# Prologue of a gated cross-attention and expert kernel: first chunk in halves, x in eight loads, one normalisation a unit sooner

## The reference, cut to what matters

```python
x = x + tanh(g_xattn) * xattn(layernorm(x), ctx, Wq, Wk, Wv, Wo, bo)     # 16 heads of 64, softmax over 128 keys
x = x + tanh(g_ffn) * ffn(layernorm(x), gate_w, gate_bias, experts, shared)
# ffn: sigmoid scores of 32 experts, best 2 of 4 groups, best 8 experts in them, weights normalised times 2.5;
#      every expert is silu(x Wg) * (x Wu), then Wd; one shared expert of twice the width is added
```

## Time and profile before

| | |
|---|---|
| runs, median of 3 | 667.44 us (667.02 to 667.79) |
| profiled execution | 668.55 us, of which the span from first to last instruction 666.8 us |
| PE busy | 650.9 us (98%) |
| DVE busy | 498.9 us (75%) |
| ACT, POOL busy | 365.3 us (55%), 284.6 us (43%) |
| granted TensorE clock | 0.999 |
| chain that ended last | PE 68%, issue 8%, DMA 6%, DVE 6%, SP's queue 5% |

### The profile page before, as it was taken

The page is one execution under the profiler, slowest core; times in us unless marked ns, Lnnn a source line. Parts: engine busy times, 40 slices in busy tenths (PEclk is TensorE's granted clock), DMA queues, the critical chain, the costliest instruction groups (busy, mean ns, idle before and its releaser), DMA issues.

```text
span 666.8 us, 13629 instructions
## 1 busy us (share of the span) xinstructions
PE 650.9 (98%) x3668; PEld 473.2 (71%) x3668; DVE 498.9 (75%) x1331; ACT 365.3 (55%) x690; POOL 284.6 (43%) x316
## 2 busy tenths in 40 slices
PE   8999999999999999999999999999999999999997
PEld 6656656667666666666657778788887878888785
DVE  6989858677586776776787968969596877869565
ACT  3564555465455555555465455555655655555553
POOL 4222323133132322234212655656565666657553
PEclk9999999999999999999999999999999999999999
DMA  8323322232323323233224825273654527374550
GB/s 188 94 64 82 92 63 70 63 91 63 80 62 79 94 62 79 62 79 83 63 67 130 192 62 134 83 170 99 141 133 98 134 72 164 81 162 112 131 142 16
DMA packets 63276, 65.58 MB, mean 98 GB/s; under 512 B 26112, under 2 KB 41600, under 8 KB 63232
## 3 DMA queue, kind: packets, MB, share of 16 engines
q1 hardware_dynamic: 63232, 65.07, 40.0%
HBM read 61.64 MB, written 2.88 MB: 97 GB/s over the span
## 4 chain that ended last, share of the span: by engine, by line
PE 68%; issue 8%; DMA 6%; DVE 6%; SPq 5%; POOL 4%; ACT 2%; DVEq 0%; POOLq 0%; ACTq 0%
PE bank L1151 13%; PE bank L1152 13%; PE bank L1153 13%; PE bank L1227 9%; PE bank L1251 5%; POOL halves L516 4%; PE bank L1187 3%; DMA inverse_bc<-inverse_dram 3%; PE bank L1207 2%; SPq L294 2%; DMA sums<-area 2%; DVE halves L783 2%; PE bank L1216 2%; PE bank L1213 2%; PE bank L1210 2%
## 5 line engine op out<-in xcount | busy, mean ns | idle before, releaser
L516 POOL TENSOR_TENSOR halves<-area,halves 128x512 fp32r<-128x512 f32 x134 | 173.9, 1298 | 141.3 <-ACT halves L650 137.8
L663 ACT ACTIVATE area<-bank 128x512 f32<-128x512 f32 x136 | 81.4, 599 | 116.1 <-PE bank L1153 115.1
L602 ACT ACTIVATE area<-bank 128x512 f32<-128x512 f32 x128 | 69.5, 595 | 118.7 <-PE bank L1216 118.7
L1107 DVE TENSOR_TENSOR bank<-area,bank 128x512 f32<-128x512 f32 x128 | 88.6, 692 | 53.4 <-PE bank L1153 53.2
L1227 PE MATMUL bank<-area,ctx_keys 128*65 128x512 f32 (+1 forms) x256 | 124.7, 600 | 0.5 <-ACT u_odd L550 0.4
L1151 PE MATMUL bank<-x2t_hi,w_hi 128*128 128x512 f32 x272 | 110.2, 405 | 0.1
L1152 PE MATMUL bank<-x2t_hi,w_lo 128*128 128x512 f32 x272 | 107.2, 394 | 0.0
L1153 PE MATMUL bank<-x2t_lo,w_hi 128*128 128x512 f32 x272 | 106.3, 391 | 0.0
L462 POOL TENSOR_TENSOR ctx_hi<-ctx_raw,ones_col 128x128 fp32r<-128x128 f32 x32 | 19.7, 615 | 200.4 <-DMA ctx_raw<-ctx_t 200.4
L792 DVE TENSOR_REDUCE row_max<-bank 128x4 f32<-128x512 f32 x128 | 81.7, 680 | 27.2 <-PE bank L1187 22.9
L650 ACT ACTIVATE halves<-area 128x512 fp32r<-128x512 f32 x136 | 85.0, 625 | 14.1 <-DVE area L1118 13.6
(11 more groups left out here) (129 smaller groups left out, 1088.1 us busy)
## 6 DMA issues: line engine op xcount, KB each, us to landing
wbc<-rows_dram SPq DMA_DIRECT2D x126, 256.0 KB, 4.4
inverse_bc<-inverse_dram SPq DMA_DIRECT2D x64, 256.0 KB, 3.9
w_raw<-experts SPq DMA_DIRECT2D x32, 102.0 KB, 2.0
ctx_raw<-ctx_t SPq DMA_DIRECT2D x32, 64.0 KB, 1.8
ctx_keys<-ctx_nat SPq DMA_DIRECT2D x32, 64.0 KB, 2.1
out<-area SPq DMA_DIRECT2D x7, 256.0 KB, 3.9
max_rows<-max_t SPq DMA_DIRECT2D x64, 4.0 KB
area<-wq_t SPq DMA_DIRECT2D x1, 512.0 KB, 4.6
```

The costliest lines, as they stand in the source:

```text
L516: nc.gpsimd.tensor_tensor(hid_lo[:, u % SLOTS, :], hid[:, u % HIDS, :], raw(hid_hi[:, u % SLOTS, :]), ALU.subtract).then_inc(hidlo_ready, 1)
L602: nc.scalar.activation(probs_t[:, k, :, :], st_ps[q][:].rearrange("p (h n) -> p h n", h=4), ACT.Exp)\
L663: nc.scalar.activation(silu_g[:, u % 2, :], gate_ps[u % 2][:], ACT.Silu).then_inc(silu_ready, 1)
L1107: nc.vector.tensor_tensor(up_ps[u % UPS][:], silu_g[:, u % 2, :], up_ps[u % UPS][:], ALU.mult)\
```

## The change

Six edits go together.

1. Layouts in DRAM: x and out are held with the partition first, so that a chunk is 2 KB in a row for each partition (before, four pieces of 512 bytes); wq and wo likewise.
2. Query and key weights come in two halves of four pairs with a semaphore each, the key half's first DMA behind the first memset alone.
3. The normalised chunk 0 goes through `apply`, transpose, `xt_high` and `xt_low` in two halves of two batches; the halves use banks 6 and 7. `g_project(0, ...)` runs banks 0 and 1, then the second half's transposes, then banks 2 and 3.
4. The first fold of value and output weights stands right behind `transpose_max(0, 0)`, the second behind its wait for `maxt_ready`; before, both stood behind `max_scores(1, ...)`. The statistics of chunk 1 are begun before the maxima of batch 1 and ended behind them. The gates' tanh and the gated bias stand behind `g_high(0, ...)` on ACT.
5. x comes in eight loads, with a semaphore each: 1 to 3 behind the router's weights, 4 behind the first two weight loads (which now stand behind the first `max_rows`), 5 and 6 in chunk 0 behind `spread_inverse(0)`, 7 behind `spread_inverse(1)`.
6. `normalise` of batch 31 moves from units 9 and 10 to units 8 and 9.

```diff
+X_AT = {1: (5, 6), 2: (7,)}
-NORM_AT = {(9, 1): ((NB - 1, 0),), (10, 1): ((NB - 1, 1),)}
+NORM_AT = {(8, 1): ((NB - 1, 0),), (9, 1): ((NB - 1, 1),)}
 fold_ps = (bank[0], bank[2])
+xt_ps = bank[6:8]
 # SP
+            def load_x(n):
+                tiles = slice(CB * n, CB * n + CB)
+                sp.dma_start(x_sb[:, tiles, :], x[:, tiles, :]).then_inc(x_in[n], 16)
-            sp.dma_start(x_sb[:, 0:CB, :], x_dram[:, 0:CB, :]).then_inc(x_in[0], 16)
-            sp.dma_start(wq_pair, wq_t.rearrange("(p r) n -> r p n", r=P)).then_inc(wqk_in, 16)
+            load_x(0)
+            for h in range(2):
+                sp.dma_start(wq_pair[:, pairs_of(h), :], wq_t[:, pairs_of(h), :]).then_inc(wqk_in[h], 16)
+                if h == 0:
+                    sp.wait_ge(zeroed, 1)
+                for q in range(2):
+                    load_diag(wk_diag, wk_t, q, pairs_of(h), wqk_in[h])
+            load_raw(0, 0)
             sp.wait_ge(zeroed, 2)
...
-            sp.dma_start(x_sb[:, CB:NB, :], x_dram[:, CB:NB, :]).then_inc(x_in[1], 16)
+            for n in range(1, 4):
+                load_x(n)
+            sp.wait_ge(const_ready, 1)
+            load_max_row(0, 0, -2)
             for slot in range(2):
                 load_weights(slot, slot * WSTEP)
-            sp.wait_ge(const_ready, 1)
-            load_max_row(0, 0, -2)
+            load_x(4)
 # SP, attention, behind spread_inverse
+                    if first:
+                        for n in X_AT.get(b, ()):
+                            load_x(n)
 # POOL
-            pool.wait_ge(x_in[1], 16)
 # ACT
             a_high(0)
-            xt_high(0)
+            xt_high_half(0)
             a_high(1)
+            g_high(0, 0, range(2))
+            xt_high_half(1)
+            g_high(0, 0, range(2, 4))
...
-            g_high(0, 0)
 # DVE
-            ln_apply(0, 0)
+            dve.wait_ge(rstd_step[0], RSTD_STEPS)
+            apply(0, 0, range(2))
             a_low(0)
-            xt_low(0)
+            xt_low_half(0)
+            apply(0, 0, range(2, 4))
             a_low(1)
-            g_low(0, 0)
+            g_low(0, 0, range(2))
+            xt_low_half(1)
+            g_low(0, 0, range(2, 4))
...
             g_low(1, 1)
+            chunk_stats_begin(1)      # waits for x_in[1]
...
-            dve.wait_ge(x_in[1], 16)
-            chunk_stats(1)
+            chunk_stats_end(1)
 # PE
-            pe.wait_ge(wqk_in, 16 * 3)
+            pe.wait_ge(wqk_in[0], 16 * 3)
             fold(wq_pair, wk_diag, 0, fold_ps[0])
             pe.wait_ge(const_ready, 6)
-            transpose_norm(0, ut_ps)
+            transpose_half(0)
+            pe.wait_ge(wqk_in[1], 16 * 3)
             fold(wq_pair, wk_diag, 1, fold_ps[1])
-            g_project(0, 0, ((glo_ready, -2), (glo_ready, -2)))
+            g_project(0, 0, None, range(2))
+            transpose_half(1)
+            g_project(0, 0, None, range(2, 4))
+            pe.wait_ge(xlo_ready, 1)
...
             transpose_max(0, 0)
+            pe.wait_ge(wvo_in, 16 * 3)
+            fold(wv_diag, wo_pair, 0, early_ps[0][0][0])
             pe.wait_ge(maxt_ready, 1)
+            fold(wv_diag, wo_pair, 1, early_ps[0][0][1])
...
-            pe.wait_ge(wvo_in, 16 * 3)
-            pe.wait_ge(max_ready, 2)
-            for i in range(2):
-                fold(wv_diag, wo_pair, i, early_ps[0][0][i])
 # host: x and out as (P, NB, D), wq and wo by pair
```

More of the change, by code:

```diff
@@ L176, in build @@
         fold_ps = (bank[0], bank[2])
+        xt_ps = bank[6:8]
         early_ps = ((bank[6:8], bank[4:6]), (bank[0:2], bank[4:6]))
         gate_ps, up_ps, route_ps, y_ps, misc_ps = bank[0:2], bank[2:5], bank[5], bank[6], bank[7]
-        x_in = [sem("x_in0"), sem("x_in1")]
-        wqk_in, wvo_in, small_in, router_in = sem("wqk_in"), sem("wvo_in"), sem("small_in"), sem("router_in")
+        x_in = [sem(f"x_in{n}") for n in range(NCH)]
+        wqk_in = [sem("wqk_in0"), sem("wqk_in1")]
+        wvo_in, small_in, router_in = sem("wvo_in"), sem("small_in"), sem("router_in")
         keys_in = [sem(f"keys_in{b}") for b in range(CB)]
@@ L530, in xt_high, with xt_high_half @@
                 nc.scalar.activation(xnt_hi[:], ut_ps[:], ACT.Copy).then_inc(xhi_ready, 1)
+            def xt_high_half(half):
+                act.wait_ge((xt_begun, xt_done)[half], 1)
+                nc.scalar.activation(xnt_hi[:, halved(half)], xt_ps[half][:, halved(half)], ACT.Copy)\
+                    .then_inc((xhi_begun, xhi_ready)[half], 1)
             def g_high(g, ring, banks=range(4)):
@@ L755, in rstd_level, with apply @@
                     ins.then_inc(stepped, 1)
-            def apply(which, t):
-                for b in range(CB):
+            def apply(which, t, batches=range(CB)):
+                for b in batches:
                     nc.vector.tensor_scalar(xn[:, b, :], tile_of(t + b),
@@ L778, in xt_low, with xt_low_half @@
                 nc.vector.tensor_tensor(xnt_lo[:], ut_ps[:], raw(xnt_hi[:]), ALU.subtract).then_inc(xlo_ready, 1)
+            def xt_low_half(half):
+                dve.wait_ge((xhi_begun, xhi_ready)[half], 1)
+                nc.vector.tensor_tensor(xnt_lo[:, halved(half)], xt_ps[half][:, halved(half)], raw(xnt_hi[:, halved(half)]),
+                                        ALU.subtract).then_inc((xlo_begun, xlo_ready)[half], 1)
             def g_low(g, ring, banks=range(4)):
@@ L1159, in transpose_norm, with transpose_half, g_project @@
                 ins.then_inc(xt_done, 1)
-            def g_project(ring, chunk, bank_free):
-                pe.wait_ge(xlo_ready, chunk + 1)
-                for j in range(4):
-                    s, value = bank_free[j // 2]
-                    wait(pe, s, value + j % 2)
+            def transpose_half(half):
+                pe.wait_ge(xn_ready, 2 * half + 2)
+                for i in range(2 * half, 2 * half + 2):
+                    ins = nc.tensor.transpose(xt_ps[half][:, i * P:(i + 1) * P], xn[:, i, :], ident[:])
+                ins.then_inc((xt_begun, xt_done)[half], 1)
+            def g_project(ring, chunk, bank_free, banks=range(4)):
+                if bank_free is None:
+                    pe.wait_ge(xlo_begun, 1)
+                else:
+                    pe.wait_ge(xlo_ready, chunk + 1)
+                for j in banks:
+                    if bank_free is not None:
+                        s, value = bank_free[j // 2]
+                        wait(pe, s, value + j % 2)
                     if j % 2 == 0:
@@ L1423, with by_pair @@
     ctx = np.asarray(ctx_512)
+    def by_pair(w):
+        return lay(np.asarray(w).reshape(PAIRS, P, D).transpose(1, 0, 2))
     def up(w, shared):
```

38 lines of the change are left out of this document (19 added, 19 removed).

## The result

| | before | changed kernel |
|---|---|---|
| median, on one chip | 667.41 us (665.59 to 668.94, 22 runs) | 668.76 us (666.92 to 671.14, 22 runs) |
| profiled execution, span | 668.55 us, 666.8 us | 671.14 us, 669.4 us |
| PE busy, DVE busy | 650.9 us, 498.9 us | 652.8 us, 500.3 us |
| granted TensorE clock of the profiled execution | 0.999 | 0.997 |
| packets of all DMAs | 63276 | 58428 |

The ratio is 1.0025, 95% interval [1.0015, 1.0035]: slower by 1.0 to 2.3 us (the medians differ by 1.35), with the forecast of 668.5 close to the median.

The account below looks back on a forecast made before the run. PE, 98% busy, was taken as the bound, with only 15.9 us idle to give back. Terms -0.3 + 2.7 - 1.2 - 0.1 = +1.1 on the 667.44 median gave 668.5 us; range 666.2 to 669.6.

Parts of the forecast that it names:

- Chunk 7's load: End of chunk 0: x load queued behind the second spread lands at 55.5, DVE waits 2.8; term +2.7 us.
- The 0.1 of slack: End of chunk 0: DVE's `take_max` of batch 5 has about 0.1 us to spare before PE's `g_project`.
- The load that lands sooner: Rival: chunk 7's load lands 2.8 us after issue, DVE waits 1.7, term +1.6, total 0.0, 667.4 us; chance 0.18.
- the wait that doesn't reach PE: Rival: DVE not held or PE's start has unseen slack; other terms stay, -1.6, 665.8 us; chance 0.10.
- Normalise: Unit 11 of the first experts: PE's wait of 1.20 for the second half goes; term -1.2 us, upper bound 0.
- The prologue: Whole prologue: PE's next product at 25.91 comes about 0.3 us sooner; -0.3, bounds -1.0 and +0.2.
- Halves: Prologue, chunk 0 in halves: 0.2 us gained up to `transpose_max`, bounds 0 and 0.5.
- The value fold and the statistics of chunk 1: Prologue: folds cover PE's 0.55 wait for `max_t`; DVE limits next, so PE's product comes about 0.3 sooner, not 0.75.
- My sign to look for: Prologue: the maxima of batch 2, h = 1, start on PE between 25.4 and 25.8 us if the forecast is right.
- x by chunks: Loads of x: chunks 1 to 6 in time, cost 0 (up to 1.0 without cover for 5 and 6); chunk 7 separate.
- Stores: Last two stores: pieces of 1 KB instead of 512 bytes may save 0.1 us; bounds -0.3 and 0.
- Payback in chunk 1: Sign against the forecast: PE's idle time in chunk 1 shrinks by as much as it grew at chunk 0's end.

## Why the prediction was right, point by point

**The total** was +1.1 forecast; measured are +1.35 by the medians and +1.0 to +2.3 by the ratio. The two large terms are the ones that the experiments bear out. That the sum comes so close is in part luck: it left out the clock (+0.5 on average) and gave the prologue and the stores 0.4 that the times don't show, and against that `normalise` gave 0.5 more in the times than forecast. I gave no change the largest chance (0.52), with 668.8 as its upper line. The median lies only 0.04 under that line, and the 22 runs tell finer than the 0.2% that I reckoned with: by their interval the change is slower.

**Chunk 7's load, +2.7.** The step was right, in its parts too: data until 54.8 forecast and 54.9 found, 0.7 more to the landing, landing forecast at 55.5, 3.9 after issue; it was 55.6, 4.2 after, in the profiled execution, and 55.3, 4.0 after, in the second. DVE's wait was 2.33 and 1.98 instead of 2.8, since DVE itself came 0.7 later than I had it (55.70 - 2.33 = 53.37 for 52.67), held by the prologue's 0.2 and the sums of batch 1. The 0.1 of slack was true: the whole wait reached PE, and the version with DVE held shows it again without any load. The load that lands sooner (1.6) and the wait that doesn't reach PE are ruled out. The estimate by the Trainium skill, "DMA: Bandwidth & Descriptors", section "Anatomy of one DMA", was 2.6 us to landing; alone in the first batch the load took 3.1, and the six late loads profiled took 4.0 to 4.8, so the measurement decides against it for a load behind two others.

**The clock** was in no step of mine. I read durations of PE in a profile at full clock, and took a pause to cost its length. In about a third of the runs it costs some 1.5 us more (1.59 in the profile, 1.5 between the medians of the runs with and without it, which may hold longer pauses as well). This is the largest thing missed; over all runs it is, as an estimate, 1.5 times 12/34, about 0.5.

**Normalise, -1.2.** Right: -1.18 in the profile, -1.7 (-0.9 to -2.3) in the times. The up product of unit 11, with its 0.15 of slack, came 0.06 late (382.92, 0.29 behind the product before it instead of 0.23). What I had not seen is that the first half takes 1.63 and not 1.22 at its new place (in the version with this edit alone as well).

**The prologue, -0.3.** The sum fits what the experiments give on average, the terms don't. Halves: forecast -0.2. `transpose_max` of batch 0 starts at 18.90 on average in the five profiled executions with chunk 0 whole (18.57 to 19.23), at 18.42 in the nine with halves (17.84 to 18.93); 0.5 sooner, though the pair first compared showed nothing (18.57 and 18.59). By the same executions the first product of `g_project` starts 0.7 sooner (10.88 for 11.58), and from there to `transpose_max` it takes 7.54 to 7.55 instead of 7.32 to 7.33: two transposes now stand in this stretch and cost about 0.2, near the 0.3 that I had. How much of the 0.7 is the halves of chunk 0, how much the weights in halves, wasn't tried apart. The value fold and the statistics of chunk 1: I took DVE for the next limit, rightly, but gave it too much room: "the same work stands ahead of that point" holds, but DVE was free to start the maxima of batch 1 at 20.41, and they now start at 21.28, behind the statistics. PE's waits of 0.55 and 0.81 become 0.38, 0.76 and 0.39. By the lengths above, the order costs 0.2 against before and 0.27 against the old order with halves; I had it as a gain of 0.1 or so. My sign to look for, maxima of batch 2 between 25.4 and 25.8, was missed by 0.3.

**The sums of batch 1** were to cost 0, as "x by chunks". They land 2.2 to 2.5 us after issue instead of 1.9: DVE waits 0.74 to 1.02 for them in all nine profiled executions with the new loads, 0.38 to 0.40 in the five without. Neither the place of chunks 5 and 6, nor the layout, nor the order of the prologue is the cause, as three experiments show. Left are the number of loads and the halves, which were not tried apart; it stays open. In the time it doesn't show, since the version with x early, which has this wait, is as fast as normalise alone.

**Stores, -0.1:** 1.7 after issue instead of 1.9 here, 1.8 with the layouts alone. The time says 1.0003, so nothing.

**Payback in chunk 1.** I had named as a sign against me that PE's idle time in chunk 1 shrinks by as much as it grew before. It does shrink: the wait for `row_max` at the end of chunk 1 (0.26 at 77.75 before) is gone, and that at the end of chunk 2 is 0.42 (103.38) instead of 1.23 (99.69). But that last wait is as small where no load is late (0.45 with x early, 0.17 with normalise alone), so this isn't the late load's payback; it was an execution of before that was itself 1.1 above its median.

**What it comes to:** normalise -1.7, chunk 7's load with the clock +3.1, all else near 0: +1.4. The kernel before with the one line for `normalise` (664.64), or the change with x early (664.69), is faster than both kernels compared; than the one before it is so by 0.25%.

## What to carry to other kernels

Ask of a load that is moved what stands in front of it: this one landed 3.1 us after issue with no spread ahead of it and 4.0 to 4.8 behind two transfers of its own size. Its reader's queue decides who pays: look for the slack of the engine that waits for that reader, here 0.1 us. Don't price a pause of PE by its length alone: from the pauses of 1.7 to 2.1 us on, here, some executions paid 1.5 us more. Read the granted clock in stretches of 2 us behind the pause, and compare several executions. When an engine is moved off a short wait, look at what the next engine in the chain was doing at that moment: a gap filled on PE (0.55) was taken from DVE, which was full.
